# Three slots and an earlier issue for the first layer's small operand, and a semaphore of its own for the band matrices

## What is computed

```python
rel = nbhd_extract(coords, 7) - coords[:, :, None, :]      # 49 neighbours of each pixel, 2 numbers each
P = jax.nn.relu(rel @ W1 + b1) @ W2 + b2                   # 64 channels
Wsm = jax.nn.softmax(P, axis=2)[0]                         # over the 49 neighbours; the same for all 8 images
V = nbhd_extract(xp, 7)                                    # zero where the window leaves the plane
out = jnp.einsum('nrc,bnrc->bnc', Wsm, V)
```

## Time and profile before

| | |
|---|---|
| median of three runs | 6821.06 us |
| the profiled execution | 6821.58 us, its span 6819.7 us |
| granted TensorE clock, mean of the span | 0.789 |
| first layer, first weight load to last window product | about 65 to 1060 us of the span |
| DVE / POOL / PE busy, share of the span | 76% / 70% / 67% |
| DMA | 853.16 MB, mean 125 GB/s |
| one load of `rel` / of a half mask / of a half window | 23.0 / 294.0 / 878.0 KB |

### The profile page before, as it was taken

One profiled execution on the slowest core, in us unless ns is written; L12 is line 12 of the kernel. 1 busy time (PEld: TensorE's weight loads), 2 busy tenths in 40 slices (PEclk: granted clock), 3 DMA queues, 4 the chain that ended last, 5 costly groups with the idle time before them and its releaser, 6 DMA issues. The chain is left out here.

```text
span 6819.7 us, 55261 instructions
## 1 busy us (share of the span) xinstructions
PE 4541.4 (67%) x14990; PEld 2454.8 (36%) x14990; DVE 5149.9 (76%) x4038; ACT 2515.4 (37%) x3865; POOL 4754.8 (70%) x3364
## 2 busy tenths in 40 slices
PE   2755765576466546633325787878888787888887
PEld 1543552233323323422222343434333343443443
DVE  2855864367666766766655898989989898998998
ACT  0111110212111101200005565666666565666664
POOL 0744752277777777777754787878878787887887
PEclk8766777575566566555557999999999999999999
DMA  3533542334443543433323444444454444444443
GB/s 115 115 73 67 115 92 63 94 104 122 124 130 104 142 131 104 136 120 105 105 87 113 147 152 142 153 139 162 141 151 149 145 148 150 150 152 142 153 151 117
DMA packets 377421, 853.16 MB, mean 125 GB/s; under 512 B 194816, under 2 KB 237720, under 8 KB 372772
## 3 DMA queue, kind: packets, MB, share of 16 engines
q1 hardware_dynamic: 292420, 618.02, 30.6%
q0 software_dynamic: 84672, 231.32, 11.2%
HBM read 766.90 MB, written 56.48 MB: 121 GB/s over the span
## 5 line engine op out<-in xcount | busy, mean ns | idle before, releaser
L2016 POOL TENSOR_TENSOR ma_hc<-ma_h,ma_cc 128x784 f32<-128x784 f32 x1024 | 1885.7, 1849 | 631.9 <-DVE ma_h L1918 497.6
L797 POOL DMA_INDIRECT fl_quad<-table,fl_idx x1764 | 1694.5, 961 | 779.0 <-issue 536.7
L1573 PE MATMUL ma_bank<-ma_hc,ident 128*128 128x392 f32 x4096 | 1530.1, 496 | 76.2 <-POOL ma_hc L2016 76.2
L1918 DVE TENSOR_TENSOR_SCAN ma_h<-ma_da,ma_state,ma_bank 128x784 f32<-128x784 f32 x768 | 1417.5, 1846 | 165.6 <-POOL ma_hc L2016 67.6
L1791 ACT ACTIVATE ma_da<-ma_dt,ma_a_neg 128x784 f32<-128x784 f32 x1024 | 948.3, 943 | 496.3 <-DVE ma_h L1918 479.5
L952 DVE TENSOR_TENSOR fl_part<-fl_quad,fl_bank 128x2304 f32<-128x2304 f32 x196 | 500.5, 2554 | 741.2 <-DMA fl_quad<-table,fl_idx 740.9
L1906 DVE TENSOR_TENSOR ma_bank<-ma_dtu,ma_bank 128x784 f32<-128x784 f32 x1024 | 981.3, 958 | 38.3 <-PE ma_bank L1560 37.6
L1094 PE MATMUL fl_bank<-ident,fl_tap 128*128 128x128 f32 (+1 forms) x980 | 245.8, 414 | 989.7 <-DVE xres L969 929.1
L1573 PEld LDWEIGHTS ma_bank<-ma_hc,ident 128*128 128x128 f32 x4096 | 711.1, 191 | 506.5 <-POOL ma_hc L2016 80.2
L1560 PE MATMUL ma_bank<-ma_bc,ma_sel 96*128 96x512 bf16 (+1 forms) x2048 | 518.9, 335 | 442.4 <-DVE ma_h L1918 430.9
L960 DVE TENSOR_REDUCE fl_tap<-fl_part 128x576 f32<-128x2304 f32 x196 | 796.4, 4063 | 0.1
(11 more groups left out here) (217 smaller groups left out, 6166.2 us busy)
## 6 DMA issues: line engine op xcount, KB each, us to landing
ma_cc<-c_rows SPq DMA_DIRECT2D x512, 784.0 KB, 4.1
mx_win<-flat SPq DMA_DIRECT2D x64, 878.0 KB, 10.4
fl_quad<-table,fl_idx POOLq DMA_INDIRECT x1764, 2.7
table<-fl_xt SPq DMA_DIRECT2D x64, 392.0 KB
mx_mask<-in_c_mask SPq DMA_DIRECT2D x56, 294.0 KB, 4.3
ma_xs<-ma_x SPq DMA_DIRECT2D x64, 196.8 KB, 5.4
ma_xs<-ma_x SPq DMA_DIRECT2D x64, 196.5 KB, 5.8
mx_xf<-flat SPq DMA_DIRECT2D x8, 816.0 KB, 15.1
```

Of the source, the lines that this page charges most:

```text
L797: gp.indirect_dma_start(quad[i][:, kk, :], None, k["tables"][q], bass.IndirectOffsetOnAxis(ap=idx[i][:, kk:kk + 1], axis=0))\
L1573: ins = pe.matmul(ps_y[:, t, :], ident[:], hc[:, n % RH, at], start=False, stop=(n == DS - 1))
L1918: dve.tensor_tensor_scan(h[:, i % RH, :], da[:, i % RH, :], ps_bu[i % 2], before, ALU.mult, ALU.add).then_inc(scand, 1)
L2016: gp.tensor_tensor(hc[:, i % RH, :], h[:, i % RH, :], cc[:, i % (NGRP * GRP), :], ALU.mult)\
```

## The change

`rel` and `w1` get a third slot, at partition 64. The load of `rel` is taken out of `load_unit`, waits for the hide three units back and is issued three units ahead. `band` gets a semaphore of its own, which TensorE awaits at the start of `uniform`. There are now 16 loads of weights and biases, and no band in their count.

```diff
-        w1 = s.sb("w1", [37, P])
+        w1 = s.sb("w1", [69, P])
-        rel = s.sb("rel", [37, NJ * COL])
+        rel = s.sb("rel", [69, NJ * COL])
...
-        rel_in = [s.sem(f"rel_in{i}") for i in range(2)]
+        rel_in = [s.sem(f"rel_in{i}") for i in range(3)]
...
-        NCONST = 2 * 6 + 1
+        NCONST = 2 * 8
...
-            def load_unit(U):
+            def load_rel(U):
+                r = U % 3
+                sp.wait_ge(hidden, START + max(U - 2, 0))
+                sp.dma_start(rel[32 * r:32 * r + 5, :], k["c_rel"][U]).then_inc(rel_in[r], 16)
+
+            def load_mask(U):
                 r = U % 2
-                sp.wait_ge(hidden, START + max(U - 1, 0))
-                sp.dma_start(rel[32 * r:32 * r + 5, :], k["c_rel"][U]).then_inc(rel_in[r], 16)
                 sp.wait_ge(masked, START + max(U - 1, 0))
...
-                for r in range(2):
+                for r in range(3):
                     sp.dma_start(w1[32 * r + 2 * h:32 * r + 2 * h + 2, own], k["W1"]).then_inc(consts, 16)
                     sp.dma_start(w1[32 * r + 4:32 * r + 5, own], k["b1"]).then_inc(consts, 16)
...
-            load_unit(0)
-            load_unit(1)
-            sp.dma_start(band[:].rearrange("p a b m -> p (a b m)"), k["c_band"]).then_inc(consts, 16)
+            for U in range(3):
+                load_rel(U)
+            for U in range(2):
+                load_mask(U)
+            sp.dma_start(band[:].rearrange("p a b m -> p (a b m)"), k["c_band"]).then_inc(band_in, 16)
             load_pair(0)
             for g in range(NG):
-                for i in range(2, KS):
-                    load_unit(KS * g + i)
+                for i in range(KS):
+                    if 3 <= i + 3 < KS:
+                        load_rel(KS * g + i + 3)
+                    if i >= 2:
+                        load_mask(KS * g + i)
                 if g < NG - 1:
                     for slot in range(2):
                         load_window(g, slot, slot)
-                    load_unit(KS * (g + 1))
-                    load_unit(KS * (g + 1) + 1)
+                    for i in range(3):
+                        load_rel(KS * (g + 1) + i)
+                    for i in range(2):
+                        load_mask(KS * (g + 1) + i)
...
             def hide(U):
-                r = U % 2
-                pe.wait_ge(rel_in[r], START + 16 * (U // 2 + 1))
+                r = U % 3
+                pe.wait_ge(rel_in[r], START + 16 * (U // 3 + 1))
...
             def uniform(g):
+                pe.wait_ge(band_in, START + 16)
                 pe.wait_ge(pair_in, START + 32 * (g + 1))
```

More of the change, by code:

```diff
@@ L298, in stage_mix @@
         vprod, gprod, reduced, kept = (s.sem(x) for x in ("vprod", "gprod", "reduced", "kept"))
-        pair_in, turned, placed, edged, restored, banded, scaled = (
-            s.sem(x) for x in ("pair_in", "turned", "placed", "edged", "restored", "banded", "scaled"))
+        pair_in, band_in, turned, placed, edged, restored, banded, scaled = (
+            s.sem(x) for x in ("pair_in", "band_in", "turned", "placed", "edged", "restored", "banded", "scaled"))
         stored = [s.sem(f"stored{i}") for i in range(2)]
```

## The result

| | before | after |
|---|---|---|
| median | 6822.37 us | 6574.13 us |
| lowest to highest (4 runs each) | 6818.94 to 6824.74 | 6569.46 to 6576.81 |
| ratio, 95% interval | | 0.9636, 0.9619 to 0.9652 |
| span of the profiled execution | 6819.7 us | 6567.7 us |
| SP's first load of the next layer (L733, after L744) | 1076.4 us | 827.2 us |

The kernel is 248 us faster; forecast were 240 us (6581 us, range 6546 to 6604). The last line of the table serves as a clock for the first layer: it ends 249.2 us earlier. The rest of the spans' difference of 252.0 us, 2.8 us, lies in later layers whose code is the same, within what the runs scatter.

A forecast was written before the change was run, and what follows sets the result against it. A chain of waits bounded the first layer's weights phases, `rel` being issued behind mask-product waits on one queue. Savings of 56.5 + 176.1 + 7.8 = 240.4 us take 6821.6 to 6581 us, range 6546 to 6604.

The forecast's parts named there:

- start (part 2): First layer's start: `hide(0)` no longer waits for the band matrices and starts near 74.9 instead of 82.74, saving 7.8 us.
- group 0, six steps (part 1): Softmax to softmax in group 0: with `rel` never last, 105.84 us fall to 49.3, saving 56.5 us.
- group 1, five steps (part 1): Softmax to softmax in group 1: 99.73 us fall to 41.0, saving 58.7 us; groups 1 to 3 alike, 176.1 us.
- tail, per group (part 3): End of each group's weights phase: the windows' issue moves as a whole and its 3 us wait stays, no gain.
- The landing of `rel`: At the first hide: `rel` taken to need 3.98 us from issue to use.
- 8.26 us: Pace per unit in the weights phases: TensorE's hide to score 4.21 us plus score to next work 4.05 us.
- I take the slow level: TensorE's clock in the weights phases: dense hides and scores assumed to stay at 1.2 GHz.
- rival A: Weights phases: TensorE gets the fast clock in dense stretches, DVE sets the pace at 6.55 us; 6546 us, chance 0.2.
- B: Weights phases: POOL's mask product and a DVE product disturb each other, or `rel` and masks meet; 6605 us, chance 0.06.
- C: Weights phases: mask loads become the loop; mild form 6620 us, chance 0.03, slow form 6832 us, chance 0.01.
- D: SP's queue: `rel` stays behind mask waits, so only the start is gained; 6814 us, chance 0.02.
- The masks' slack: SP's mask loads: issued 16.5 us before their product, landing in a median 4.3 us, leaving about 9 us.

The follow-up runs named there:

- old order with three slots: Changed kernel with three slots and band's own semaphore, but each `rel` load again just ahead of its own mask, behind the mask before it: 6826.5 us, ratio 0.9998.
- semaphores per bank: Changed kernel with `scored` and `shifted` counted per bank of the score, so TensorE and DVE wait bank by bank: 6562.9 us, ratio 0.9625.
- the combined kernel: Changed kernel plus side-by-side hide products, per-bank score semaphores, softmax without b2, each group's first windows early, first pair behind unit 4's `rel`: 6526.7 us, ratio 0.9567.
- the next two remedies: Each alone on the changed kernel: a hide's three products side by side, 6572.1 us; score semaphores counted per bank, 6562.9 us.
- the two together: Changed kernel with a hide's three products side by side and score semaphores counted per bank: 6560.7 us, ratio 0.9617.
- the later runs: Ending in: changed kernel, side-by-side hides, per-bank semaphores, softmax without b2, windows early except group 0, first pair behind unit 4's `rel`: 6520.7 us, ratio 0.9553.
- no addition: Kernel with side-by-side hides and per-bank score semaphores, without DVE's addition of b2 to the maximum: 6538.8 us, ratio 0.9582.

## Why the prediction was right

Point by point, by its own steps, in the first layer:

| step of the prediction | said | measured |
|---|---|---|
| start (part 2) | 7.8 us | 8.9 us (first softmax 96.88 to 87.94) |
| group 0, six steps (part 1) | 56.5 us | 58.8 us (105.84 to 47.01) |
| group 1, five steps (part 1) | 58.7 us | 60.2 us (99.73 to 39.53) |
| tail, per group (part 3) | 0 | 1.0 and 0.7 us |
| whole layer | 240.4 us | 249.2 us |

From first window product to first window product the three later groups gained 60.9, 59.6 and 60.0 us.

*The cause.* It was the order of the queue, and the old order with three slots gave the loss back but for 4.9 us. The title of the change names three slots first; the third is worth 4 us in this order, all of it at the start.

*The start.* The landing of `rel` was mis-sized: 3.98 us from issue to use in the earlier trace rows, 2.65 us here (71.05 to 73.70). The row of before has a pair of masks issued just ahead of it; here nothing but small loads is. The weight load just ahead of that hide is put down to the last of the constants (issued at 70.41), so 2.65 us is a bound on the landing of `rel`; which of the two ended the wait is open. In the other direction I had not seen that an early start by the semaphore alone would be eaten by a late third `rel`: old order gained 4.9 us, not 9. In the change it was not, because that `rel` goes out ahead of the masks.

*The pace.* 8.26 us was said, 7.8 to 7.9 us came. The step that failed is "I take the slow level": of the 20 hides of units 2 to 6 in the four groups 12 ran in 2.2 to 2.6 us. It cost the forecast little, for the reason given against rival A, that a fast hide only lets TensorE wait for the softmax. There was luck in it: two loops of nearly one length were there, 8.26 us of TensorE and 7.8 us of the score buffer, and the listing of part 1 had both; the kernel switches between them.

*The rivals.* A came by half: 12 hides got the fast level, but no score ran at it throughout; the shortest of the 28 took 3.66 us, and with such scores the loop of score, softmax and next score over one buffer took 7.35 us or more, so DVE was not the bound. With a whole score at the fast level (2.24 us in the kernel with semaphores per bank, at 95.16) that loop would be about 2.3 + 3.4 = 5.7 us, an estimate, and DVE would have been next. Even then the figure of A was wrong: 7.54 us is DVE's own pace in that order, since an instruction of 0.24 us is held for 1.3 by POOL. That price stood in no row of before, where the two never met. So the disturbance between POOL and DVE that B names is real, but it cost next to nothing at 7.8 us a unit. B, C and D did not come, and D's mechanism is what the old order made. The masks' slack held; a wait for a mask that costs time was seen only in the combined kernel, where windows stood ahead of it.

*The bound of the time.* The remaining 8.8 us over the forecast are thus 1.1 at the start, 2.3 in the steps of group 0, 1.5 in those of group 1, and the rest in groups 2 and 3 and the tails.

## What to carry to other kernels

One in-order queue turns unlike waits into one: a load that needs nothing of a wait should be issued ahead of it, and before a buffer is added it is worth asking what the load stands behind. Put large transfers behind small urgent ones of the same moment, and count megabytes ahead of each, at the start of a phase above all. When one bound goes, list the loops just under it with their lengths: two of them here lay within half a microsecond, so the next two remedies gave 5 and 14 us of the first layer, the two together 15, and 56 us only with what the later runs added.

## What the runs showed of the hardware

**An addition on DVE (tensor_scalar) waited for a POOL instruction under way; the reductions didn't.** On 24 numbers a partition in SBUF it took 1.31 us when a product of POOL (2.66 us, two operands in SBUF) had started before it, and ended with it; 0.24 us otherwise. The changed kernel has it already, where only the end of the product is met (DVE, then POOL, which ends at 128.75):

```profile
128.36 0.42 DVE L550 TENSOR_SCALAR mx_topb<-mx_top,mx_b 128x24 f32<-128x24 f32 x1
```

```profile
126.09 2.66 POOL L616 TENSOR_TENSOR mx_wts<-mx_wts,mx_mask 128x1176 f32<-128x1176 f32 x1 [5.70 <-DVE mx_wts L566]
```

The three maxima of PSUM took 1.50 us and the three subtractions from PSUM 1.69 either way. A product of two tensors in SBUF on DVE took 2.35 us in place of 1.38 when it met POOL's (no addition, at 132.28). The Trainium skill (SBUF — State Buffer, Who interferes with whom) says that `tensor_scalar` can take the port pair that DVE shares with GpSimd, that whoever comes second blocks until the other ends, and that `tensor_reduce` never contends; these rows agree. That it was the port pair they can't show, only who waited for whom.

**A hide behind a score that was fast at its end ran fast; a hide and a score in a row can run slow throughout.** In the weights phases of the changed kernel all six hides behind a score of less than 4.25 us took 2.24 us; of the 14 behind a score of 4.26 to 4.29 us six took 2.3 to 2.6 us and eight 4.28 or 4.29. Over the score of 3.67 us at 99.20 the granted clock was 0.60, over the hide behind it 1.00. The table of stages for two short stretches of the changed kernel (columns as in rows 1), for the earlier trace rows: 

```profile
96.80:98.60 1.80, 0.87 (x3) 0.18 (x1) 1.73 (x5) 0.00 (x0) 0.00 (x0) 1.00 0.00 0
291.40:299.70 8.30, 8.30 (x13) 3.63 (x12) 6.41 (x10) 2.22 (x2) 3.00 (x2) 0.50 0.29 73
```

In the second TensorE had no pause for 8.3 us (hide 4.29, score 4.29) and the granted clock was 0.50, the level of 1.2 GHz; in the first, with a fast hide just over, it was 1.00, 2.4 GHz. So how dense TensorE's work was did not alone tell the level here, in the changed kernel as in the one before. What does was not settled by these runs.

**Products at partitions 0, 32 and 64 ran together:** six passes in 1.68 us in place of 4.28 at the slow clock and 0.93 in place of 2.24 at the fast one.
